# Differential attention with one full-height matmul pair per score tile, doubled queries and a shorter batch edge

## What is computed

```python
q, k, v = x @ wq.T, x @ wk.T, x @ wv.T            # wq, wk: 1024 x 512
# 8 heads; each has two sub-heads of 64 columns for q and k, one v of 64
scores = einsum('bhqd,bhkd->bhqk', q, k) / 8      # 16 sub-heads, causal mask
attn = softmax(scores)
attn = attn[:, :8] - attn[:, 8:] * lmbda          # first minus second sub-head
out = rms_norm_in_groups_of_8(attn @ v) @ wo.T
ffn = fwht(silu(x @ W1.T) * (x @ W3.T)) @ W2.T    # 2048 hidden units
```

## Time and profile before

| | us |
|---|---|
| median of 3 runs | 3775.64 (3774.65 to 3775.76) |
| the profiled execution's own time | 3770.78 |
| its span | 3769.0 |
| PE busy | 3183.8 (84%) |
| DVE busy | 1951.8 (52%) |
| POOL busy | 1859.7 (49%) |
| ACT busy | 1364.2 (36%) |
| granted TensorE clock, mean | 0.94 |

### The profile page before, as it was taken

One profiled execution on the slowest core, in us unless ns is written; L12 is line 12 of the kernel. 1 busy time (PEld: TensorE's weight loads), 2 busy tenths in 40 slices (PEclk: granted clock), 3 DMA queues, 4 the chain that ended last, 5 costly groups with the idle time before them and its releaser, 6 DMA issues. The chain is left out here.

```text
span 3769.0 us, 46728 instructions
## 1 busy us (share of the span) xinstructions
PE 3183.8 (84%) x16049; PEld 2443.1 (65%) x16049; DVE 1951.8 (52%) x3951; ACT 1364.2 (36%) x2989; POOL 1859.7 (49%) x1707
## 2 busy tenths in 40 slices
PE   2899999899999979999989999995888983088776
PEld 0677777677777767777767777773776762044443
DVE  6355556645565655655664556565544655811110
ACT  2344444344444424444443444443323321022221
POOL 3256667646576645765773657654222241033333
PEclk9899999999999999999999999997998986589998
DMA  5211111321111141110123111103121111099897
GB/s 156 83 37 43 40 37 43 106 71 45 31 43 45 40 134 40 40 48 29 40 84 98 43 37 40 42 21 121 54 70 67 58 64 60 18 266 246 240 245 177
DMA packets 251183, 301.99 MB, mean 80 GB/s; under 512 B 19664, under 2 KB 168016, under 8 KB 250320
## 3 DMA queue, kind: packets, MB, share of 16 engines
q1 hardware_dynamic: 236624, 263.49, 22.3%
q0 software_dynamic: 14336, 35.66, 4.5%
HBM read 233.46 MB, written 65.57 MB: 79 GB/s over the span
## 5 line engine op out<-in xcount | busy, mean ns | idle before, releaser
L799 ACT ACTIVATE probs<-score_ps,neg_max 128x640 f32<-128x640 f32 (+7 forms) x512 | 374.4, 738 | 363.0 <-DVE neg_max L660 362.5
L690 POOL TENSOR_TENSOR probs<-probs 128x512 f32<-128x512 f32 (+3 forms) x384 | 383.4, 1013 | 10.7
L685 POOL TENSOR_SCALAR probs<-probs,comb 128x512 f32<-128x512 f32 (+3 forms) x384 | 230.0, 607 | 309.2 <-DVE comb L596 301.3
L660 DVE TENSOR_REDUCE neg_max<-score_ps 128x2 f32<-128x256 f32 (+7 forms) x256 | 346.5, 1353 | 58.9 <-PE score_ps L915 55.2
L694 POOL TENSOR_TENSOR out_root<-out_root,neg_half 128x16 f32<-128x16 f32 x128 | 371.8, 2907 | 5.7 <-DVE out_root L630 5.7
L552 DVE TENSOR_TENSOR layer_sum<-product_ps,layer_sum 128x512 f32<-128x512 f32 x384 | 262.4, 684 | 44.7 <-PE product_ps L61 41.6
L912 PE MATMUL score_ps<-keys_all,queries_all 64*128 64x512 f32 (+3 forms) x2304 | 277.2, 363 | 0.0
L539 DVE TENSOR_TENSOR attT<-turn_ps,attT 128x512 fp32r<-128x512 f32 (+3 forms) x384 | 211.6, 551 | 84.5 <-ACT attT L720 84.3
L720 ACT ACTIVATE attT<-turn_ps 128x512 fp32r<-128x512 f32 (+3 forms) x384 | 188.2, 490 | 142.8 <-PE turn_ps L825 142.8
L912 PEld LDWEIGHTS score_ps<-keys_all,queries_all 64*128 64x128 f32 x2304 | 187.8, 185 | 74.0 <-issue 44.7
L59 PE MATMUL product_ps<-xT_hi,w_up 128*128 128x512 f32 x512 | 211.6, 413 | 28.3 <-DVE queries_all L559 20.2
(11 more groups left out here) (248 smaller groups left out, 7676.3 us busy)
## 6 DMA issues: line engine op xcount, KB each, us to landing
e_gate_up<-in_w_gate_dram SPq DMA_DIRECT2D x64, 384.0 KB, 4.0
e_gate_up<-in_w_up_dram SPq DMA_DIRECT2D x64, 384.0 KB, 5.4
e_down<-in_w_down_dram SPq DMA_DIRECT2D x64, 384.0 KB, 6.8
w_stage<-in_wqk_dram SPq DMA_DIRECT2D x64, 256.0 KB, 3.1
w_stage<-in_w1T_dram SPq DMA_DIRECT2D x64, 256.0 KB, 2.6
w_stage<-in_w3T_dram SPq DMA_DIRECT2D x64, 256.0 KB, 2.7
values_by_head<-hidden_split SPq DMA_DIRECT2D x32, 512.0 KB, 3.2
w_stage<-w_transformed SPq DMA_DIRECT2D x64, 256.0 KB, 2.7
```

Source lines behind the costliest of these rows:

```text
L660: dve.tensor_reduce(nmax[:, i % 2, :], score_tile(i % NT), AX.X, ALU.max, negate=True)\
L685: pool.tensor_scalar(PR[:, r, 1, c], PR[:, r, 1, c], comb[:, i % 4:i % 4 + 1], 1.0, ALU.mult, ALU.mult)\
L690: pool.tensor_tensor(PR[:, r, 0, c], PR[:, r, 0, c], PR[:, r, 1, c], ALU.add).then_inc(s_comb, 1)
L799: act.activation(PR[:, i % 2, q, 0:(j + 1) * P], score_tile(j)[:, q, :], ACT.Exp, bias=nmax[:, i % 2, q:q + 1], accum_out=sums[:, i % 16, ...
```

## The change

Three parts. **Scores:** the keys' hi and lo halves are stacked on the partitions (for sub-head 0, hi on 0 to 63 and lo on 64 to 127; for sub-head 1 the other way round), still double-buffered. The queries' hi and lo halves each lie on all 128 partitions, twice the same; they are no longer double-buffered. A block of keys takes four 128-row matmuls: (q_hi, q_lo) for each sub-head, which also adds the lo·lo product. To make the layout, each projected quarter takes two ACT and two DVE instructions on 64 partitions in place of one and one on 128, and SP copies each half of the queries to the other partitions with two DMAs (256 KB each). The last query quarter is projected one step later, at step 8h of the head that uses it.

**Order of the step:** PE runs gate_up, values, turn_map 0, (x turn), down, fold, pair turn, scores, turn_map 1, (V), output, project. DVE, ACT and `gb` are reordered to match.

**Edges:** 11 slots. A new buffer holds x tiles 0 to 2, loaded three steps before the batch ends. Tile t is turned in slot t+1 and gets its V in slot t+2; DVE normalises it at the end of slot t. The last slot projects three quarters.

```diff
-    HEAD_SLOTS, TAIL_SLOTS = 13, 10
+    HEAD_SLOTS, TAIL_SLOTS, EARLY = 11, 10, 3
+        XE = sb("x_early", [P, EARLY, D])
...
+            if not 0 <= i < STEPS or i % 2:
+                return None
+            h, q = (i // NT, 3) if i % NT == 0 else (i // NT + 1, i % NT // 2 - 1)
+            return (h, q) if h < HEADS else None
...
+                def double_queries(b, h, half):
+                    done, c = query_quarter(b, h, half)
+                    sp.wait_ge(s_gbfree, done)
+                    for q, here, there in ((0, lo64, hi64), (1, hi64, lo64)):
+                        v = Q[:, q, :, c].bitcast(F32)
+                        sp.dma_start(v[there], v[here]).then_inc(s_qd[half], 16)
...
+                    if hb and s == -EARLY:
+                        sp.wait_ge(s_xtf, (hb - 1) * NT + EARLY)
+                        for t in range(EARLY):
+                            load_x(hb, t)
+                    if hb and s in (0, 1):
                         sp.wait_ge(s_ttf, tt[b, i, 1] + 1)
-                        for t in range(4 * s, 4 * s + 4):
+                        for t in range(EARLY + 4 * s, min(NT, EARLY + 4 * s + 4)):
...
+                    if b is not None and i < STEPS and proj_at(i - 1) and proj_at(i - 1)[1] % 2:
+                        double_queries(b, proj_at(i - 1)[0], proj_at(i - 1)[1] // 2)
+                    if hb is not None and s == HEAD_SLOTS - 1:
+                        double_queries(hb, 0, 0)
...
                 def proj_low(b, h, q):
...
+                    raw = gbank("P", b, h, q)
+                    for sub, here, there in ((0, lo64, hi64), (1, hi64, lo64)):
+                        if q % 2:
+                            ins = dve.scalar_tensor_tensor(Q[here, sub, 1, c], raw[here, :], 0.125, Q[here, sub, 0, c].bitcast(F32),
+                                                           ALU.mult, ALU.subtract)
+                        else:
+                            ins = dve.tensor_tensor(K[there, r, sub, c], raw[here, :], K[here, r, sub, c].bitcast(F32),
+                                                    ALU.subtract)
...
                 def proj_high(b, h, q):
...
-                    if q % 2:
-                        ins = act.activation(Q[:, r, 0, c], gbank("P", b, h, q), ACT.Copy, scale=0.125)
+                    for sub, here in ((0, lo64), (1, hi64)):
+                        if q % 2:
+                            ins = act.activation(Q[here, sub, 0, c], raw[here, :], ACT.Copy, scale=0.125)
...
                     if j in (0, 4):
-                        pe.wait_ge(s_gbfree, gb["P", b, hd, 1 if j == 0 else 3] + 1)
+                        pe.wait_ge(s_gbfree, gb["P", b, hd, j // 2] + 1)
+                        pe.wait_ge(s_qd[j // 4], 32 * (b * HEADS + hd + 1))
...
-                        for m, (qp, kp) in enumerate(((0, 0), (1, 0), (0, 1))):
-                            for q, rows in enumerate((lo64, hi64)):
-                                pe.matmul(score_bank(q, j, c0)[:, 0:w], Q[rows, r, qp, j * P:(j + 1) * P],
-                                          K[rows, r, kp, c0:c0 + w], start=(m == 0), stop=(m == 2 and c0 + w < n))
+                        for q in range(2):
+                            for part in range(2):
+                                pe.matmul(score_bank(q, j, c0)[:, 0:w], Q[:, q, part, j * P:(j + 1) * P],
+                                          K[:, r, q, c0:c0 + w], start=(part == 0), stop=(part == 1 and c0 + w < n))
...
+                        if i < STEPS:
+                            gate_up(b, i)
                         g = group_at(i)
                         if g is not None:
                             values(b, g)
                         if has_turn(i):
                             turn_map(b, i, 0)
-                    if hb is not None and 3 <= s < 3 + NT:
-                        t = s - 3
+                    if hb is not None and 1 <= s < 1 + NT:
+                        t = s - 1
...
-                        if i < STEPS:
-                            gate_up(b, i)
+                        if has_down(i):
+                            down(b, i)
...
-                    if hb is not None and 4 <= s < 4 + NT:
-                        t = s - 4
+                    if hb is not None and 2 <= s < 2 + NT:
+                        t = s - 2
...
+                        if pair_at(i):
+                            output(b, i)
                         if proj_at(i):
                             project(b, *proj_at(i))
-                        if pair_at(i):
-                            output(b, i)
                     if hb is not None and s == HEAD_SLOTS - 1:
-                        for q in range(4):
+                        for q in range(3):
                             project(hb, 0, q)
```

191 lines of the change are left out of this document (96 added, 95 removed).

## The result

The changed kernel takes 3801.72 us (median of 6 runs, 3796.78 to 3816.12), against 3771.99 for the kernel before on the same chip: ratio 1.0089 [1.0072, 1.0107]. It is slower by 0.9%, where 3690 was forecast. The interval lies clear of 1, so the loss is not noise.

What follows compares the result with a forecast made beforehand. PE was taken as the bound in the steps, with idle time at start and edges. Scores -4, order -18, edges -40 and start -24 made -86 on 3770.8, so 3685, with 4.9 for the median 3690; range 3640 to 3760.

Steps and rivals of the forecast that it cites:

- Start and edges: Batch start and three edges: 11 slots and earlier x normalisation give -24 us at the start, -40 at the edges.
- Scores: Score matmuls on PE: a fourth slot costs 67 us, fixed time given back 64; put at -4, bounds -25 and +61.
- the fixed 0.20: Old 64-row score block on PE: 0.20 us from first matmul to mask that doesn't grow with the pairs.
- nothing given back: Rival on scores: the fixed 0.30 belongs to the block, not its shape; +65, 3755 us, chance 0.13.
- the 0.30: Fixed time around a 64-row score block, inside it and at the turn ahead; 0.25 x 256 = 64 us back.
- Making the layout: Projected quarters: 77 us more on ACT, 89 on DVE, beside PE, counting only where a bank is awaited.
- the 20.2 of waits called gone: PE's waits for the projected queries' low halves, 20.2 us in 24; the shorter ones covered by gate_up's 2.85.
- New order: Steps of a batch: 14 idle us for 18.4, -18 us over four batches, bounds -60 and +40.
- The loop comb, POOL, `pow`, norm product, comb: Rival in pair-head steps: this chain becomes the bound, 10.3 us a step for 9.0; +125, 3833 us, chance 0.10.
- the order removes nearly all idle: Rival on the steps: -55 for -18, and scores -20 for -4; 3637 us, chance 0.10.
- three signs of being wrong: Pair heads over 80 us; POOL's pow chain as PE's wait; copies later than 8 us with scores waiting inside a batch.
- The copies: Doubling DMAs of queries on SP: 4 us for two, free inside a batch, about 2 us at each batch's first step.

Runs made afterwards that it cites:

- single instructions: One ACT and one DVE instruction a quarter (wrong scores): 3735.89 on the changed kernel, 3681.78 there with comb early, 3778.43 on full-height scores in old order and edges.
- comb early: Reciprocal and comb ahead of DVE's norm product: 3732.39 for new order on the kernel before, 3669.82 with new edges too, 3769.67 on the changed kernel.
- the same two in the old order: Kernel before with full-height scores alone: with one ACT and one DVE instruction a quarter 3778.43 us, with the key weights one step later 3910.73.

## Why the prediction was wrong, point by point

The result is some 116 us above the forecast change (+30 for -86). By the parts taken alone, the scores with their layout make 65 of it (+61 for -4), the order 47 (+29 for -18), and start and edges 5 (-59 for -64).

**Start and edges: right in mechanism, edges mis-sized.** First scores were forecast at 133.5 and came at 132.5. An edge was to fall from 90.5 to 75 and fell to 81. PE's waits for x are gone, as forecast. Mis-sized is what stays: "about 5 stays in the chains of the first slots", with V and the copies 9 idle, where 81.0 - 67.5 = 13.5 is; 7.5 of it lies in four waits of the first slots (2.89, 1.70, 1.12 and 1.80), the first of them:

```profile
1323.61 2.82 PE L927 MATMUL pv_ps<-attT,values 128*128 128x256 f32 x12 [2.89 <-DVE attT L566]
```

The other 1.5 is in PE's busy time (67.5 for 66), with a clock of 0.87 for 0.96. In sum it matters little: the two terms gave -64, and the edges alone measured -59.

**Scores: right, with some luck in the terms.** -4 was forecast in bounds of -25 and +61. Its working gives 67 - 64 = +3; the step from there to -4, by "the rounding of the measured blocks", has no row behind it. The sums with single instructions put the scores at +8 (old order) and +12 (new order with comb early), copies and moved quarter included; in PE's busy time they come to about nothing (see the same two in the old order). Blocks of 128, 512 and 896 keys, against the earlier trace rows:

```profile
825.71 0.64 PE L947 MATMUL score_ps<-keys_all,queries_all 128*128 128x128 f32 x4
826.19 0.29 PE L950 MATMUL score_ps<-maskb,identb 128*128 128x128 bf16 x2
...
849.82 1.07 PE L947 MATMUL score_ps<-keys_all,queries_all 128*128 128x512 f32 x4
850.73 0.29 PE L950 MATMUL score_ps<-maskb,identb 128*128 128x128 bf16 x2
...
872.63 1.88 PE L947 MATMUL score_ps<-keys_all,queries_all 128*128 128x512 f32 x8
874.36 0.28 PE L950 MATMUL score_ps<-maskb,identb 128*128 128x128 bf16 x2
```

A full block of 512 keys takes 0.91 to its mask, as four slots of 0.228; before, it took 0.89 for three pairs. 896 keys take 1.73, where the slots make 4 x (0.228 + 0.174) = 1.61. So most of the fixed 0.20 inside the block was given back, and the rival "nothing given back" is out. 1024 keys take 1.83 to 1.95, where 1.85 was said. But a block of 128 keys takes 0.48, not 0.3, and so does one of 256: the slot of a narrow matmul is 0.12 (0.48 / 4), not the 0.062 that the width gave. The small turn ahead of the scores, 0.21 to the next start in the earlier trace rows, is down to 0.05 here (0.12 at the start of that head):

```profile
964.22 0.30 PE L859 MATMUL turn_ps<-ident_sb,heads_out 128*128 128x128 f32 x1 [0.33 <-DVE attT L566]
964.27 0.95 PE L947 MATMUL score_ps<-keys_all,queries_all 128*128 128x512 f32 x3
```

So most of the 0.30 came back. The rule of the Trainium skill that a change of the tiling mode drains the engine (TensorEngine Tiling (Array Packing), Key Properties) fits these rows, though no run shows the drain itself. The same page's speedup for a contraction of 64 rows (Theoretical Speedup) is there inside a block, two 64-row matmuls in 0.23; that giving it up would cost +61 isn't borne out here.

**Making the layout: this is the first step that failed.** The instructions were priced rightly (0.60 and 0.69 on half the partitions; `down` waits 1.08 in a pair head where "about 1" was said, up to 1.9 in light ones where 1.4 was). It waits for the keys and not, as forecast, for the queries, since the shifted projections put the keys' second quarter at j = 6. The sentence that failed is "It counts only where a bank is awaited", with nothing in the sum. Even by its own figures something was missing there: a new wait of 1.4 in the four light heads of each batch that project for the next is 22 us (16 x 1.4), which the 20.2 of waits called gone could at best have offset. It counts +66 in the new order, +154 in the old, +88 with comb early. The lo halves stand first in DVE's step, so 0.7 more there, and 0.6 ahead of it on ACT, is 1.3 more for the head output, the norm product, the hidden product and map_low, all of which a bank of PE hangs on. That DVE was busy 46 of 76 us said nothing about it: DVE idles in waits for ACT and POOL and is late all the same. It was weighed against one bank only. A light head takes 68.9 and a pair head 79.0, where 66 and 75 were forecast.

**New order: the second.** -18 was forecast, +29 measured. values' wait for attT went as forecast (28.4 to 11.2, of which one a batch is left, at the edge), but the turns' wait for the same bank grew (16.4 to 47.6). The loop comb, POOL, `pow`, norm product, comb was found, and priced at "10 us at the worst and 8.5 on average against PE's 9.0 a step"; from root to root it shows 9.46 at j = 6, of which DVE's part is 3.4 for the 3.1 estimated. It was taken for a near miss with slack, and DVE then waited 49.9 us for `pow` with the order alone (1.4 before). As a rival it had 0.10, with 10.3 us a step and +125; the truth is smaller in each step, but comes with the clock and with the small DVE instructions that lengthen where POOL is late, neither of which that rival had. With comb early the order gives -42, between the forecast -18 and the -55 of the rival "the order removes nearly all idle". The question to ask of the diff was why comb should stand behind the norm product at all: it needs neither that nor the add of `down`.

**The clock in the steps: missing.** 54.6 us at the lower level for the order alone, 75.1 in the changed kernel. The same idle time costs more where it lies together: 17.9 us in a batch's steps with the clock at 0.99, where 18.4 cost nothing. That there are two levels was plain from the start's 0.87, but only there did the clock enter the sum. None of the three signs of being wrong that the prediction named came: pair heads stay under 80, `pow` shows as DVE's wait and not as PE's, and the copies land in time. A wait of PE's own was the wrong place to look for this loop.

The Trainium skill (TensorE: Matmul & The Clock Gate, A second HAM failure mode) tells of a bf16 kernel whose PE stops shortly and often between groups of matmuls, goes back and forth between the two clocks, and pays for it between bursts. The rows at 906 and 912.5 agree; the steps of before, with as much idle time at 1.00, show that stops alone don't do it.

**The copies: right.** They land after 3.7 us (median of 128, the longest 5.3; bounds were 2 and 8). Inside a batch no scores wait for them. At a batch's first step they do, as forecast: four times 1.3 to 1.4 us, for the 2 us said. The profile puts the waits down to DVE's hidden product or to nothing, but in all four batches the second copy lands 0.09 us before the first scores start (here at 132.39).

```profile
127.96 1.34 SPq L493 DMA_DIRECT2D queries_all<-queries_all  x2
...
132.48 0.63 PE L947 MATMUL score_ps<-keys_all,queries_all 128*128 128x128 f32 x4 [1.40 <-DVE hidden L641]
```

## What to carry to other kernels

An engine that idles for 40% of the time can still be late: before adding work at the head of its step, follow every later instruction of that engine whose result a bank or a chain waits for, and price the delay, not the busy time. When an order is rewritten, look for loops over engines (here comb, POOL, norm product) and keep what needs nothing of the loop ahead of it; two instructions of 0.15 and 0.2 us decided between -42 and +29. Take a change of several parts apart on the chip: here one part alone was the better kernel.

## What was not expected of the hardware

- On ACT and DVE half the partitions take the full time: 593 and 689 ns for 64x512 on ACT and DVE, against 595 ns and 0.69 us for 128x512. The forecast took this as an assumption with bounds; now it is shown. The Trainium skill's picture of VectorE as independent lanes that stream along the free dimension (VectorE: DVE Perf Modes, Why `tensor_reduce` can't reduce along partition axis) agrees.
- The score matmuls of 128 rows follow each other at about 0.12 us for 128 as for 256 columns, and so the blocks of 128 and of 256 keys both take 0.48 to the mask.
- The granted clock falls to 0.51 within a full-speed stretch, after PE worked 3.84 of 6.40 us; for 3.4 us ten matmuls run at half speed. The same sum of idle time over a batch's steps, spread out, left it at 1.00.
- The same small DVE instruction is recorded with 0.28 us where POOL does nothing and with 0.81 to 1.38 where POOL makes the lo half of a hidden unit (the norm product, 48 and 52 cases in order alone); the root argument with 0.19 and 1.19.
- Doubled instructions of 166 us (77 on ACT, 89 on DVE) cost 88 us with comb early, though ACT is busy for 48% and DVE for 59% of the steps (260.55 and 321.88 of 545.40).
